# The experts' first weights: from a table in SBUF that VectorE copies, to tiles that SyncE loads from DRAM

## What is computed

```python
x = x + xattn(ctx, layernorm(x))     # 16 heads: softmax(q k^T) v, residual, layernorm
x = x + ffn(layernorm(x))
# ffn, for each of the 3200 rows:
z = layernorm(x); probs = softmax(z @ rW + rb)            # 8 experts
w = top-2 of probs, divided by their sum
hid = gelu(z @ W1[e] + b1[e])                             # 256 -> 512
mixed = sum over the two chosen e of w_e * (hid @ W2[e] + b2[e])   # 512 -> 256
return x + mixed
```

## Time and profile before

| | us |
|---|---|
| median of three executions | 837.0 (833.88 to 838.32) |
| the profiled execution's own time | 831.98 |
| its span, first to last instruction | 830.1 |
| PE busy over the span | 748.1 (90%) |
| DVE busy | 629.8 (76%) |
| ACT busy | 564.5 (68%) |
| POOL busy | 535.6 (65%) |
| packets of SP's queue (q1) / of POOL's (q0), share of the 16 DMA engines | 43.7% / 10.6% |
| data moved by DMA in the second part | 50 to 76 GB/s a slice, the last 25 |

### The profile page before, as it was taken

How to read it: one execution, slowest core, us unless ns; L and a number is a source line. 1 busy time by engine, 2 the same in 40 slices (tenths; PEclk the granted TensorE clock), 3 DMA queues, 4 the chain that set the end, 5 groups by cost and what they waited for, 6 DMA issues and landing times.

```text
span 830.1 us, 26296 instructions
## 1 busy us (share of the span) xinstructions
PE 748.1 (90%) x8080; PEld 584.2 (70%) x8081; DVE 629.8 (76%) x1781; ACT 564.5 (68%) x1469; POOL 535.6 (65%) x609
## 2 busy tenths in 40 slices
PE   7888989999999999999999997545979887999995
PEld 4556666767777777777777674435968787999995
DVE  7688998988999999999999897793446773454542
ACT  3466777878888888888888885443655553666663
POOL 5433757777777767768767665336466555677773
PEclk9999999999999999999999999755989998999998
DMA  8566775777687786787786867711334332433432
GB/s 215 148 145 156 153 157 121 167 169 162 155 190 153 164 181 141 182 162 158 170 171 150 190 143 180 207 11 50 52 57 63 52 51 53 76 62 62 62 66 25
DMA packets 154000, 104.43 MB, mean 126 GB/s; under 512 B 68364, under 2 KB 149560, under 8 KB 153816
## 3 DMA queue, kind: packets, MB, share of 16 engines
q1 hardware_dynamic: 135502, 79.47, 43.7%
q0 software_dynamic: 10944, 14.10, 10.6%
q10 hardware_dynamic: 7498, 10.18, 4.1%
HBM read 36.65 MB, written 17.33 MB: 65 GB/s over the span
## 4 chain that ended last, share of the span: by engine, by line
PE 57%; DVE 11%; DMA 11%; POOL 7%; issue 6%; SPq 5%; ACT 2%; DVEq 1%; ACTq 0%; POOLq 0%
PE s_row L1015 10%; PE pj L910 7%; PE s_row L924 7%; PE pj L879 6%; PE zt L956 6%; PE s_t L944 6%; PE pj L1026 4%; PE zt L1026 4%; SPq L668 3%; DMA stack_x<-in_x 2%; DVE negmax L1401 2%; DMA zscr<-zn 2%; PE pj L897 2%; DMA stack_x<-k_part 2%; DMA z_in<-zscr 1%
## 5 line engine op out<-in xcount | busy, mean ns | idle before, releaser
L1401 DVE TENSOR_REDUCE negmax<-s_row 100x1 f32<-100x361 f32 x512 | 251.2, 523 | 21.7 <-PE s_row L924 17.2
L1220 ACT ACTIVATE p_t<-s_t 128x400 f32<-128x400 f32 x384 | 187.9, 499 | 80.9 <-PE s_t L944 73.0
L924 PE MATMUL s_row<-stack_x,q_stack 125*128 125x361 bf16 x512 | 132.0, 318 | 16.8 <-DVE negmax L1401 9.6
L944 PE MATMUL s_t<-q_stack,stack_x 128*128 128x100 bf16 x1536 | 128.3, 210 | 11.4 <-ACT p_t L1220 8.5
L740 POOL DMA_INDIRECT out_x<-index_space,idx_s x56 | 90.1, 1609 | 71.1 <-DMA out_x<-index_space,idx_s 26.3
L944 PEld LDWEIGHTS s_t<-q_stack,stack_x 128*128 128x128 bf16 x1536 | 93.7, 99 | 56.0 <-issue 31.0
L1015 PE MATMUL s_row<-w_qkv,v_aug 128*128 128x128 f32 x912 | 117.7, 285 | 0.5 <-DVE v_aug L1496 0.5
L1015 PEld LDWEIGHTS s_row<-w_qkv,v_aug 128*128 128x128 f32 x912 | 112.7, 201 | 0.9 <-DVE v_aug L1496 0.8
L1406 DVE TENSOR_SCALAR p_t<-p_t 128x1200 f32<-128x1200 f32 x128 | 100.9, 788 | 11.2 <-ACT p_t L1220 11.1
L910 PE MATMUL pj<-w_qkv,ct 128*128 128x256 f32 x384 | 104.8, 395 | 0.3 <-ACT k_rest L1141 0.3
L956 PE MATMUL zt<-p_t,v_aug 128*32 128x100 f32 (+1 forms) x3072 | 95.6, 258 | 0.9 <-DVE p_t L1406 0.8
(11 more groups left out here) (247 smaller groups left out, 1414.0 us busy)
## 6 DMA issues: line engine op xcount, KB each, us to landing
stack_x<-k_part SPq DMA_DIRECT2D x192, 192.0 KB, 3.6
q_stack<-q_part SPq DMA_DIRECT2D x192, 64.0 KB, 2.0
ct<-in_ctx_t SPq DMA_DIRECT2D x32, 361.0 KB, 4.4
stack_x<-in_w ACTq DMA_DIRECT2D x8, 512.0 KB, 6.2
w_s<-in_w ACTq DMA_DIRECT2D x14, 256.0 KB, 3.0
zscr<-zn SPq DMA_DIRECT2D x32, 100.0 KB
z_in<-zscr SPq DMA_DIRECT2D x32, 100.0 KB
zf_d<-zf_s SPq DMA_DIRECT2D x32, 100.0 KB
```

The costliest lines, as they stand in the source:

```text
L924: nc.tensor.matmul(s_row[h % 2][:, 0:KEYS], q_stack[0:MROW, b.slot, h, :], k_stack[0:MROW, b.slot, h, 0:KEYS], start=True, stop=True).then ...
L944: last = nc.tensor.matmul(s_t[g % 2][:, j * Q:j * Q + Q], k_stack[:, b.slot, h, kt * 128:kt * 128 + 128], q_stack[:, b.slot, h, 0:Q], star ...
L1220: nc.scalar.activation(p_t[:, quad % 2, kt, :], s_t[g % 2][:, 0:4 * Q], ACT.Exp).then_inc(exp_done, 1)
L1401: v.tensor_reduce(negmax[:, b.slot, h:h + 1], s_row[h % 2][0:Q, 0:KEYS], AXIS.X, ALU.max, negate=True).then_inc(max_done, 1)
```

## The change

The table, its loads, both copies and the register load before them are gone. The host now lays out weights and bias of one expert as 128 rows of 1028 numbers (4112 bytes). SP reads the tile's expert from `te_i`, waits until the gelu of the tile that had the slot is done (k-4), and loads the 526 KB of the expert into slot `k % 4` of a new buffer. The first four loads stand at place 387, and the one of tile k+4 stands in SP's `tile_step(k)`, which SP did not have before. PE waits for the load's semaphore, one for each slot. The gate's copy on DVE gets one more wait (`y_ready`), on the result of four tiles earlier. In `first_tiles` DVE no longer waits for the table's loads and for the last batches' values.

```diff
@@ -180,11 +180,9 @@
-        b1_s = sb(es, "b1_s", [128, E, 4])
-        route_const, rw_scaled, shift_done, rb_shifted, b1_loaded = (sem(k) for k in (
-            "route_const", "rw_scaled", "shift_done", "rb_shifted", "b1_loaded"))
+        route_const, rw_scaled, shift_done, rb_shifted = (sem(k) for k in ("route_const", "rw_scaled", "shift_done", "rb_shifted"))
-        w1_s = sb(es, "w1_s", [128, 2, E, HF])
+        w1_k = sb(es, "w1_k", [128, 4, 2 * HF + 4])
@@ -193,7 +191,7 @@
-        w1_loaded = sem("w1_loaded")
+        w1_copied = [sem(f"w1_copied{k}") for k in range(4)]
@@ -547,18 +545,15 @@
-            w1_k = [v_aug[:, k].rearrange("p n w -> p (n w)")[:, 0:2 * HF] for k in (2, 0)]
             gate = sb(att, "gate", [128, 4])
-            b1_k = sb(att, "b1_k", [128, 2, 4])
-            zgt_done, zgt_copied, up_done, b1_ready, gelu_done = (sem(k) for k in ("zgt_done", "zgt_copied", "up_done", "b1_ready", "gelu_done"))
+            zgt_done, zgt_copied, up_done, gelu_done = (sem(k) for k in ("zgt_done", "zgt_copied", "up_done", "gelu_done"))
             gate_ready, y_biased, down_done, y_ready = (sem(k) for k in ("gate_ready", "y_biased", "down_done", "y_ready"))
-            w1_copied = sem("w1_copied")
 
@@ -624,7 +619,16 @@
                 def later_loads():
                     for dst, src in zip(row_c, (gamma, beta)):
                         sp.dma_start(dst[:], src.unsqueeze(0).broadcast_to([Q, D])).then_inc(tail_const, 16)
-                    sp.dma_start(b1_s[:], b1).then_inc(b1_loaded, 16)
+
+                def load_w1(k):
+                    sp.wait_ge(tiles_known, 2 if k.known and k.index >= NF else 1)
+                    e = sp.value_load(te_i[0:1, bass.ds(k.index, 1)], min_val=0, max_val=E - 1)
+                    after(sp, gelu_done, 4 * (k.index - 3))
+                    sp.dma_start(w1_k[:, k.ring], w1[bass.ds(e, 1)].rearrange("e p f -> p (e f)")).then_inc(w1_copied[k.ring], 16)
+
+                def tile_step(k):
+                    if not k.known or k.index + 4 < NT:
+                        load_w1(k.later(4))
 
                 def iteration(turn, i):
                     if isinstance(turn, int) and i == 0:
@@ -678,9 +682,15 @@
                         for group in range(2):
                             if at(f"store{group}"):
                                 store_gates(sp, group)
+                        if at("w1"):
+                            for c in range(4):
+                                load_w1(Tile(0, c))
+                        for k in tiles_at(turn, i, s):
+                            tile_step(k)
 
                 pipeline(sp, iteration, last=9)
 
+                remaining(sp, tile_step, LOOP[0])
                 for k in range(3):
                     sp.wait_ge(zf_stored[k], 16 * len(range(k, B, 3)))
 
@@ -1007,13 +1017,13 @@
                     return pe.value_load(te_i[0:1, bass.ds(k.index, 1)], min_val=0, max_val=E - 1)
 
                 def up(k):
-                    pe.wait_ge(w1_copied, k.index + 1)
+                    pe.wait_ge(w1_copied[k.ring], 16 * k.turn + 16)
                     pe.wait_ge(zgt_copied, k.index + 1)
                     after(pe, gelu_done, 4 * (k.index - 1))
                     for j in range(4):
                         for c in range(2):
                             last = nc.tensor.matmul(p_h[k.slot][:, j * 128:j * 128 + 128],
-                                                    w1_k[k.slot][:, c * HF + j * 128:c * HF + j * 128 + 128],
+                                                    w1_k[:, k.ring, c * HF + j * 128:c * HF + j * 128 + 128],
                                                     zgt[:, k.slot, c * 128:c * 128 + 128], start=(c == 0), stop=(c == 1))
                     last.then_inc(up_done, 1)
 
@@ -1171,8 +1181,6 @@
                     act.dma_start(w2_s[:, e], w2[e].rearrange("(c p) f -> p c f", p=128)).then_inc(w2_loaded, 16)
 
                 def load_weights(i):
-                    if i == 27:
-                        act.dma_start(w1_s[:, :, E - 1, :], w1[E - 1].rearrange("(c p) f -> p c f", p=128)).then_inc(w1_loaded, 16)
                     if i == 30:
                         act.wait_ge(x2_stored, 16 * LOOSE)
                         for e in range(3, E):
@@ -1193,11 +1201,10 @@
 
                 def gelu(k):
                     act.wait_ge(up_done, k.index + 1)
-                    act.wait_ge(b1_ready, k.index + 1)
                     after(act, down_done, k.index - 1)
                     for j in range(4):
                         nc.scalar.activation(hidt[:, k.slot, j * 128:j * 128 + 128], p_h[k.slot][:, j * 128:j * 128 + 128], ACT.Gelu,
-                                             bias=b1_k[:, k.slot, j:j + 1]).then_inc(gelu_done, 1)
+                                             bias=w1_k[:, k.ring, 2 * HF + j:2 * HF + j + 1]).then_inc(gelu_done, 1)
 
                 def gated(k):
                     act.wait_ge(y_biased, k.index + 1)
@@ -1242,9 +1249,6 @@
                         at = moment(turn, i, s)
                         for a in due(turn, i, s, 3, "ACT", "q"):
                             queries_high(a)
-                        if not isinstance(turn, int) and i < 2 and s == 5:
-                            act.dma_start(w1_s[:, i, bass.ds(turn - 2, 1), :].rearrange("p e f -> p (e f)"),
-                                          w1[bass.ds(turn - 2, 1), i * 128:i * 128 + 128, :].rearrange("e p f -> p (e f)")).then_inc(w1_loaded, 16)
                         n, g = lagging(turn, i, s, SCORES_LAG)
                         if n.valid():
                             exponentials(n, g)
@@ -1487,16 +1491,9 @@
                     dve.wait_ge(zgt_done, k.index + 1)
                     v.tensor_tensor(zg[:, k.ring, D + 1:D + 2], zg[:, k.ring, D + 1:D + 2], zg[:, k.ring, D:D + 1], ALU.subtract).then_inc(gate_ready, 1)
                     dve.wait_ge(gate_ready, 2 * k.index + 1)
+                    after(dve, y_ready, k.index - 3)
                     v.tensor_scalar(gate[:, k.ring:k.ring + 1], second[:, bass.ds(k.index, 1)], zg[:, k.ring, D + 1:D + 2], zg[:, k.ring, D:D + 1],
                                     ALU.mult, ALU.add).then_inc(gate_ready, 1)
-
-                def weights(k):
-                    e = dve.value_load(te_i[0:1, bass.ds(k.index, 1)], min_val=0, max_val=E - 1)
-                    after(dve, up_done, k.index - 1)
-                    v.tensor_scalar(w1_k[k.slot].rearrange("p (c f) -> p c f", c=2), w1_s[:, :, bass.ds(e, 1), :].rearrange("p c e f -> p c (e f)"),
-                                    1.0, None, ALU.mult).then_inc(w1_copied, 1)
-                    after(dve, gelu_done, 4 * (k.index - 1))
-                    v.tensor_scalar(b1_k[:, k.slot], b1_s[:, bass.ds(e, 1), :].rearrange("p e f -> p (e f)"), 0.0, None, ALU.add).then_inc(b1_ready, 1)
 
                 def result(k):
                     e = dve.value_load(te_i[0:1, bass.ds(k.index, 1)], min_val=0, max_val=E - 1)
@@ -1511,7 +1508,6 @@
                     if not k.known or k.index >= 1:
                         result(k.later(-1))
                     if not k.known or k.index + 2 < NT:
-                        weights(k.later(2))
                         gating(k.later(2))
                     if not k.known or k.index + 6 < NF or NF - 3 < k.index < NT - 6:
                         to_gather(k.later(6))
@@ -1521,11 +1517,6 @@
 
                 def first_tiles():
                     dve.wait_ge(w2_loaded, N_W2)
-                    dve.wait_ge(w1_loaded, 16 * (2 * E - 1))
-                    dve.wait_ge(pv_done, G * (B - 1))
-                    dve.wait_ge(b1_loaded, 16)
-                    weights(Tile(0, 0))
-                    weights(Tile(0, 1))
                     for c in range(2):
                         gating(Tile(0, c))
                         to_gather(Tile(0, c + 4))
...
-               "lanes01": 382, "lanes02": 383, "lanes03": 384, "gates0": 374, "store0": 379, "picks0": 385, "experts0": 386, "index0": 386, "gather": 391,
+               "lanes01": 382, "lanes02": 383, "lanes03": 384, "gates0": 374, "store0": 379, "picks0": 385, "experts0": 386, "w1": 387, "index0": 386, "gather": 391,
...
-WEIGHT_LOADS = (27, 30, 31)
+WEIGHT_LOADS = (30, 31)
...
-        "w1": p["ffn_W1"], "b1": np.ascontiguousarray(p["ffn_b1"].reshape(E, 4, 128).transpose(2, 0, 1)), "w2": p["ffn_W2"], "b2": p["ffn_b2"],
+        "w1": np.concatenate([p["ffn_W1"].reshape(E, 2, 128, HF).transpose(0, 2, 1, 3).reshape(E, 128, 2 * HF), p["ffn_b1"].reshape(E, 4, 128).transpose(0, 2, 1)], 2), "w2": p["ffn_W2"], "b2": p["ffn_b2"],
```

More of the change, by code:

```diff
@@ L155, in pipeline, with build @@
         iteration(0, i)
-def build(nc, x, ctx_t, wq_t, bq, wk_t, bk, wv_t, bv, gamma, beta, ln_g, ln_b, rw, rb, w1, b1, w2, b2,
+def build(nc, x, ctx_t, wq_t, bq, wk_t, bk, wv_t, bv, gamma, beta, ln_g, ln_b, rw, rb, w1, w2, b2,
           ident_d, route_c, zscr, zf_d, out):
```

## The result

The changed kernel takes 844.3 us in the median (839.3 to 847.4), the kernel before 835.7 us in the same comparison: ratio 1.0111, 95% interval 1.009 to 1.0133. By the ratio it is slower by 9.3 us (the medians stand 8.6 apart), where I forecast 6 us faster. The time lies in the range given, the sign is wrong.

A forecast was written before the change was run, and what follows sets the result against it. PE was taken as the limit in attention and late tiles, waiting only in the middle stretch. The terms -9.3 - 1.0 + 1.7 + 2.5 = -6.1 us, laid on the 837.0 median, gave 831 us, range 821 to 847.

The forecast's parts named there:

- The scatters against the new loads: Tile stage: the new loads lengthen scatter landings; together +2.5 us, from 0 to +22.
- Late it is even, +0.5: Late tiles: with four tiles for an expert, GpSimd's mean of 3.72 us matches PE's 3.73; +0.5 us.
- D: What the loads add to a scatter's landing: between 0 and 1.6 us, taken as 0.6.
- Beside the routing, +1.5: Middle stretch, 16 tiles: longer landings bring back 2.6 us, of which slack takes a part; +1.5 us.
- rival 1: Scatters set the pace: about 850 us if landings grow by 2 us, 840 at D 1.2; chance 0.22.
- The relief of DVE, -9.3: Middle stretch: without DVE's copies most of PE's idle and slow-clock time goes; -9.3 us, from -2 to -15.
- -1.0 for GpSimd: Start of the tile stage: gathers no longer held up by DVE's copies; -1.0 us, from 0 to -1.4.
- what is late next is as late: Lower end of DVE's relief in the middle stretch: the next late thing holds PE as long; only -2 us.
- SP's order around batch 31, +1.7: `z_in` stands behind the loads of tiles 4 and 5, so batch 31's rows land later; +1.7 us, -1 to +4.
- rival 4: SP's loads come late for `up`, PE waits at tiles 8 to 10: about 838 us; chance 0.06.
- Attention: 0: Attention: the dropped table loads were hidden behind a busy PE; 0 to -1 us, taken as 0.
- the 16 periods: Sign of the forecast: the 16 tile periods after batch 31's gap take under 72 us, where before 78.1.

The follow-up runs named there:

- f1: The changed kernel with loads from tile 24 on cut to the bias columns, so old weights there: 832.84 us, ratio 0.9967 to the kernel before.
- e1: The changed kernel with loads from tile 4 on cut to the 4 bias columns (2 KB for 526 KB), old weights: 826.35 us, ratio 0.9936.
- g1: The changed kernel with four result buffers and index columns in place of two: 834.89 us, ratio 1.0034 to the kernel before.
- f3: The changed kernel with SP's loads of tiles 4 and 5 put behind `z_in`, batch 31's rows: 845.97 us, ratio 1.0105.
- e4: The changed kernel with each load cut into four DMAs of 257 columns (rows of 1028 bytes, not 4112): 843.31 us, ratio 1.0122.
- g4: The changed kernel with loads from tile 4 on bringing 516 of 1028 columns (264 KB of 526), half the weights old: 830.26 us, ratio 0.9982.
- g3: The kernel before with loads for tiles 4 to 23, DVE's copies for the others, and four result buffers: 827.94 us, ratio 0.9953.
- f2: The changed kernel with loads of tiles 4 to 23 cut to the bias columns, whole loads later: 837.09 us, ratio 1.0028.
- e3: The changed kernel with the load of tile k (k from 6) held until scatter k-6 has landed: 843.57 us, ratio 1.0143.

## Why the prediction was wrong

**The step that failed: "The scatters against the new loads", its term "Late it is even, +0.5".** The form of the sum was right: late, GpSimd's queue sets the pace, with one long step at a change of expert and short ones between. Both sizes in it were wrong. I took 4.66 + 0.6 = 5.26 us for the long step, and it measured 5.66. I took four tiles for an expert, and between tiles 27 and 50 there are 3.3. With my own 5.26 and 3.2 us and the real number of changes the mean is 3.83 us, which isn't even with PE's 3.73; with the measured steps it is 3.97, and 4.01 was measured. Over 33 tiles the 0.28 us more than PE's pace are 9 us, the +9.1 of the late section (12 by f1), where I had 1.0 with the end. For D I had no row with a scatter beside a large load and took the lower part of its bounds. It came out at 0.8 for the median landing (3.8 to 4.6 us), and at 1.4 for the steps that GpSimd waits in (4.27 to 5.66).

**Beside the routing, +1.5 in the same sum: measured 4.1 (e1's 74.8 to 78.9).** DVE waits for the landing of scatter k-2 at every tile. The earlier trace rows showed it with 29.3 us, and I used that row only as a hint for rival 1. With two buffers more the 4.1 us are gone (g1).

**The relief of DVE, -9.3 with -1.0 for GpSimd: measured 5.3 us (e1).** Of the waits of PE for ACT's scaled rows 1.5 of the 5.0 us stayed without the loads (e1) and 3.5 with them; the one for ACT's table stayed (2.2 and 2.8, of 2.4). For the most part only DVE's idle time grew. I had "what is late next is as late" for the lower end alone. The stretch beside the routing did give 5.4 us in e1 (80.2 to 74.8) and in g1, and 1.3 with loads and two buffers.

**SP's order around batch 31, +1.7.** The size fits (PE's gap 5.2 to 8.1 us; 2.2 us in the section) and the mechanism doesn't. `z_in` did go out 4.3 us later (589.49 against 585.16 in the earlier trace rows), but 3.4 of that is the later start of the stage, and f3 moved it ahead for nothing. The first scatter, beside the loads of tiles 4 and 5, landed late.

**Right.** The load's landing (4.2 us for an expected 4.4), in time for `up` everywhere: rival 4 fell. The GpSimd gathers: the mean went from 1191 to 1092 ns, where I had said all near 1.03 us. By the Trainium skill, "SBUF — State Buffer", section "SBUF: two separate sides", it is DVE's two-port copy that holds GpSimd's descriptors up, and the trace agrees. DMA share late 0.79 for 0.8. Attention: 0, by e1.

**The other rule weighed.** The Trainium skill, "DMA: Bandwidth & Descriptors", section "Queues, rings and completion order", has each engine go round its queues packet by packet. I took a row of the load for a packet. The section counts some 9 to 17 descriptors to a packet, so e4, which shortens the rows, is no clean test of the rule. D at the long steps, 1.4, is near the 1.6 that I worked out by it, and 1.0 in e4; the time didn't follow (1.0122). The runs neither show the rule at work nor speak against it.

**The rivals.** Rival 1 named the right place and the right mechanism, and its sign came: the scatters across a change of expert stand 5.1 to 6.3 us apart, 5.66 in the mean, where it asked for over 5.6. PE's `down` doesn't wait for DVE's result, its other sign. It asked for D over 0.9 because it too counted four tiles for an expert; with 3.3 PE's pace bears 4.80 us, which is D = 0.14 on its 4.66. So its price of 840 us at D = 1.2 was too small. (Its 850 us for D = 2 is 18 us laid on the profiled execution; laid on the median, as the forecast is, that would be 855.) The chances were off with it: 0.22 for what happened. Of the signs of the forecast, PE still waits 3.5 us for the scaled rows, and the 16 periods take 76.6 us (617.09 to 693.72), not under 72.

**Still open.** That the long steps are the changes of expert is read from the kernel's waits and the traces; no run took the wait at a change away. Of the 3.4 us by which the first `up` came later in the profile after, a part is clock. Near 470 us PE idles 1.55 us in both, waiting for DVE's `negmax`; then, of the changed kernel and of e1 (last three numbers: granted clock, DMA share, GB/s):

```profile
475.00:480.00 5.00, 5.00 (x30) 4.00 (x32) 2.95 (x9) 3.47 (x10) 3.54 (x6) 0.50 1.01 246
```

```profile
475.00:480.00 5.00, 5.00 (x77) 3.37 (x75) 4.28 (x11) 3.77 (x12) 3.49 (x5) 1.00 1.04 199
```

The one went on at the lower clock level, the other at the higher. Among the profiles of kernels that share the changed attention the first `up` lies between 575.4 and 579.9 us, among those that share the old one between 574.2 and 579.1. Why one execution falls and another does not I did not find. How the remaining cost in g1 (1.0034 against e1's 0.9936) splits between the wait at a change of expert and the gathers' own longer landings was not tried.

## What to carry to other kernels

When a copy on an engine is replaced by a transfer, price the transfer by what it does to the other transfers that someone waits for, at the places where they are waited for, and count these places. Here the median landing grew by 0.8 us, the steps in which GpSimd waits for one grew by 1.4, and such a step came every 3.3 tiles and not every four. Write each queue's mean with these numbers beside the pace of the limiting engine: nothing happens until it is passed (g4), and then every tile pays. Look also for short buffer loops: a wait of an engine off the critical path for a landing (here 29 us on DVE) is where longer landings enter beside the routing. And an engine made lighter gains only as far as the buffers in front of it allow: beside the routing the relief was worth 5.4 us without the loads, 1.3 with them, and 5.4 again with two more buffers.

## What the runs showed of the hardware

- An indirect scatter of 128 rows landed in 3.8 us (median) with no load beside it (g3), 4.0 beside 258 KB per tile (g4) and 4.6 beside 514 KB per tile (g1), with a DMA share of 0.39, 0.60 and 0.78. A gather landed in 2.9, 3.2 and 4.6 us in the same profiles.
- The second scatter of the stage, which waits for the first one's landing, started 7.84 us behind it with two whole loads beside them, 5.78 with two halves (g4) and 4.77 with two small ones (f2).
- Cutting those loads into rows a quarter as long (e4) or issuing them at another moment (e3) made no difference to the time outside the intervals (1.0122 and 1.0143 against 1.0111). In their profiles the steps over a change of expert were 5.23 and 5.17 us, for 5.66.
- The same idle spell of PE, 1.55 us, was followed by the lower clock level in one execution and not in another.
